# Capsule passes 2 and 3 of a graph network: half of the step sums added by VectorE from PSUM, and another layout of a chunk's edges

## What is computed

```python
xc = l2norm(x.reshape(num_node, 8, 16))
z = xc[src]
u = xc
for _ in range(3):
    p = einsum('ecd,ecd->ec', z, u[trg])
    p = softmax(p, axis=1)
    msg = z * p[:, :, None]
    u = segment_sum(msg, trg, num_segments=num_node)
    u = l2norm(u + xc)
```

## Time and profile before

| what | value |
|---|---|
| median of 3 runs | 6134.75 us (6134.14 to 6145.96) |
| span of the profiled execution | 6133.4 us |
| median less that span | 1.35 us |
| `CAPS2` and `CAPS3` in it | from 3089 to 4062 us of the span, 488 steps |
| POOL busy over the span | 4562.7 us (74%) |
| PE busy | 3912.3 us (64%) |
| DVE busy | 3726.0 us (61%) |
| ACT busy | 1638.9 us (27%) |

### The profile page before, as it was taken

One profiled execution on the slowest core, in us unless ns is written; L12 is line 12 of the kernel. 1 busy time (PEld: TensorE's weight loads), 2 busy tenths in 40 slices (PEclk: granted clock), 3 DMA queues, 4 the chain that ended last, 5 costly groups with the idle time before them and its releaser, 6 DMA issues. The chain is left out here.

```text
span 6133.4 us, 123500 instructions
## 1 busy us (share of the span) xinstructions
PE 3912.3 (64%) x27584; PEld 3400.1 (55%) x27585; DVE 3726.0 (61%) x9157; ACT 1638.9 (27%) x4058; POOL 4562.7 (74%) x5214
## 2 busy tenths in 40 slices
PE   1555555555555477777789989956566665666665
PEld 1544444455455366666578878845555553555553
DVE  6333333565666677777887787775555555555555
ACT  1000000112121333333455565531111113222222
POOL 6777777677777677777778888857777776777776
PEclk9666666666666688888899999977777776888887
DMA  4222222222222355555577777732222222222222
GB/s 124 68 70 68 70 69 68 62 69 68 70 68 70 103 175 171 172 170 171 169 231 248 249 226 248 249 109 69 69 69 69 70 68 54 71 71 71 69 71 95
DMA packets 447304, 697.73 MB, mean 114 GB/s; under 512 B 89485, under 2 KB 204570, under 8 KB 446282
## 3 DMA queue, kind: packets, MB, share of 16 engines
q0 software_dynamic: 127616, 263.32, 16.6%
q10 hardware_dynamic: 210816, 255.92, 12.8%
q1 hardware_dynamic: 108746, 177.24, 9.1%
HBM read 506.58 MB, written 189.53 MB: 113 GB/s over the span
## 5 line engine op out<-in xcount | busy, mean ns | idle before, releaser
L759 POOL DMA_INDIRECT u_parts<-table,src x3128 | 2951.6, 944 | 1063.2 <-issue 952.1
L835 PE MATMUL ps_sum<-u_parts,onehot 128*128 x2928 | 655.5, 395 | 691.6 <-SPq L588 552.2
L1374 DVE SCALAR_TENSOR_TENSOR onehot<-dst,minus_row,beside 128x512 f32<-128x512 f32 x1100 | 816.9, 744 | 365.7 <-issue 308.6
L835 PEld LDWEIGHTS ps_sum<-u_parts,onehot 128*128 128x128 f32 x2928 | 573.7, 291 | 776.2 <-issue 775.4
L759 POOL DMA_INDIRECT ring<-table,src x782 | 746.2, 954 | 264.9 <-issue 237.7
L835 PE MATMUL ps_u<-u_parts,onehot 128*128 x2928 | 535.9, 343 | 515.6 <-SPq L588 452.2
L835 PEld LDWEIGHTS ps_sum<-msg,onehot 128*128 128x128 f32 x4896 | 693.7, 213 | 306.8 <-issue 149.1
L835 PE MATMUL ps_sum<-msg,onehot 128*128 128x128 f32 x4896 | 753.9, 303 | 127.0 <-DVE msg L457 96.9
L835 PEld LDWEIGHTS ps_u<-u_parts,onehot 128*128 128x128 f32 x2928 | 473.0, 246 | 566.0 <-issue 565.0
L1669 DVE TENSOR_TENSOR zu<-ps_u,ring 128x512 f32<-128x512 f32 x732 | 502.7, 687 | 351.7 <-SPq L588 192.6
L885 PE MATMUL ps_u<-u_parts,hots 128*128 x5856 | 487.9, 235 | 56.2 <-ACT hots L1144 39.4
(11 more groups left out here) (205 smaller groups left out, 6477.8 us busy)
## 6 DMA issues: line engine op xcount, KB each, us to landing
ring<-z_rows SPq DMA_DIRECT2D x392, 256.0 KB, 3.5
hot_rows<-hots ACTq DMA_DIRECT2D x244, 256.0 KB
hots<-hot_rows ACTq DMA_DIRECT2D x244, 256.0 KB, 3.4
z_rows<-ring SPq DMA_DIRECT2D x196, 256.0 KB, 2.1
u_parts<-table,src POOLq DMA_INDIRECT x3128, 2.5
table<-hots ACTq DMA_DIRECT2D x122, 256.0 KB
wide<-hot_rows ACTq DMA_DIRECT2D x122, 256.0 KB, 3.4
wide_t<-hot_rows ACTq DMA_DIRECT2D x122, 256.0 KB, 3.5
```

The costliest lines, as they stand in the source:

```text
L759: nc.gpsimd.indirect_dma_start(out=slot(p, c % slots)[:, t * P:(t + 1) * P], out_offset=None, in_=tables[p], in_offset=bass.IndirectOffset ...
L835: last = nc.tensor.matmul(sums[k % len(sums)][:, 0:P], lhsT=(onehot[:, k % HOTS, :, :] if hots_of is None else hots_of)[:, t, :], rhs=rows ...
L1374: V.scalar_tensor_tensor(out=buffers[k % len(buffers)], in0=per_row(dst[:, ds(chunk * TILES, TILES)], [P, TILES, P]), scalar=minus_row0[:, ...
```

## The change

Of the step sums of `CAPS2` and `CAPS3`, POOL keeps the even steps (`pool_adds`). The odd ones are added by DVE straight from PSUM with `add_step`, in the even iterations, seven iterations behind (`lag` 3 becomes 7). ACT copies only the even sums and raises `sum_out` by 2; PE waits for `sum_out` before it refills an even bank, for `step_added` before an odd one. POOL's wait for the start of a piece of `x` now covers step s+1 too.

Apart from that, the host lays out a chunk's edges by tiles: edge number t·128 + p of a chunk goes to tile t, partition p, where before edge 4·p + t did. The last chunk holds 160 edges and gathers 2 tiles.

```diff
+        def pool_adds(k):
+            return k % 2 == 0
...
-                    if have(3):
+                    if have(3) and pool_adds(k - 3):
                         add(s.back(3), k - 3, chunk(3))
...
-                    if s.fixed and (s + 0) % PIECE == 0 and s + 0 < PIECES * PIECE:
-                        pool.wait_ge(acc_started, PIECES + thirds_before(m, (s + 0) // PIECE + 1))
+                    for first in (s + 0, s + 1) if s.fixed else ():
+                        if first % PIECE == 0 and first < PIECES * PIECE:
+                            pool.wait_ge(acc_started, PIECES + thirds_before(m, first // PIECE + 1))
...
-                                 step_added if p == CAPS1 else sum_out,
+                                 sum_out if p > CAPS1 and pool_adds(k - lag) else step_added,
...
-                    if have(4):
+                    if have(4) and pool_adds(k - 4):
                         act.wait_ge(step_summed, s + (G - 3))
                         act.wait_ge(step_added, s + (G - 7))
                         nc.scalar.activation(sums_out[k % len(sums_out)], four_sums[k % len(four_sums)][:, 0:P],
-                                             ACT.Copy).then_inc(sum_out, 1)
+                                             ACT.Copy).then_inc(sum_out, 2)
...
-                lag = SUM_LAG[p] + 2 if p == CAPS1 else 3
+                lag = SUM_LAG[p] + (2 if p == CAPS1 else 3)
...
+                    if p != CAPS1 and have(lag) and not pool_adds(k - lag):
+                        add_step(s.back(lag), k - lag, chunk(lag), p, caps_sums[p])
                     if s.fixed and s + 0 < STEPS:
                         piece_work(s, p)
...
-        return padded.reshape(CHUNKS, P, -1).transpose(1, 0, 2).reshape(P, -1)
+        return padded.reshape(CHUNKS, TILES, P).transpose(2, 0, 1).reshape(P, -1)
...
-        "attr": attr.reshape(CHUNKS // RING, RING, P, TILES * D_EDGE).transpose(0, 3, 1, 2)
+        "attr": attr.reshape(CHUNKS // RING, RING, TILES, P, D_EDGE).transpose(0, 2, 4, 1, 3)
```

## The result

The changed kernel takes **6150.7 us** (median of 10 runs, 6148.89 to 6151.71). The kernel before took 6135.52 beside it: ratio 1.0024, 95% interval 1.0016 to 1.0032, so slower by 15 us. The forecast was 6161, slower. The direction and the range held; the time was forecast 10 us too high.

A forecast was written before the change was run, and what follows sets the result against it. The loop was taken to be bound by a circle over prob_n, first message, PE, zu and reciprocal, without POOL's adds. Terms -7.0 + 5.6 + 9 + 7.0 + 7.5 + 4.7 = +26.8 us gave 6161; range 6110 to 6180, own case 6147 to 6178.

The forecast's parts named there:

- POOL's relief, loops: Loops of CAPS2 and CAPS3: fewer POOL adds help the slower circle 0.42 and 0.08 in 24 steps, -7.0 us.
- adds and table load at DVE's tops: At 28 tops of DVE's loop: adds 0.20 each, +5.6 us, and the longer table load 0.25 each, +7.0 us.
- adds, changes of passes: Where passes change DVE is 95% busy and has no gaps: 52 adds, 10.4 in full, taken as +9 us.
- loads, written-out rounds: Outside the loops 34 table loads grow from 8 to 12 values, and CAPS3 gets one more: +7.5 us.
- end of CAPS3: DVE must add step 243 before the next layernorm's statistics and 4.78 us of work: +4.7 us, bounds 3 and 5.
- slower circle: One of two interleaved circles of even and odd pairs, prob_n to reciprocal to prob_n: 6.90 us for four steps.
- On the slower circle this helps only where POOL was late: Loops: POOL's shorter pair gains only 0.42 at one pair and 0.08 at another in 24 steps, -7.0 us.
- the rival on POOL's pace: Loops: POOL sets the pace, 6 of 12 pairs gain 0.41 each, 35 us; total 6112 us, chance 0.21.
- Some lie behind a piece instruction: +7.5 of 9.4: Written-out rounds: some longer table loads hide behind a piece instruction on DVE, so +7.5 us of 9.4 counts.
- all exposed: Upper end of the forecast's own range, all adds and loads exposed and POOL's relief nothing: 6178 us.
- The adds hold each other: Rival: POOL's and DVE's alternating adds wait in order, 0.3 each on 244 adds, 73 us more: 6230 us, chance 0.05.
- The port: Rival: DVE's adds slow POOL's messages, 0.5 us each on 244, about 6250 us, chance 0.03.

The follow-up runs named there:

- e1: Changed kernel with the CAPS3 adds from step 236 on given back to POOL, run again on another chip: 7515.04 us against 7505.87 before, ratio 1.0013.
- a1: Kernel before with POOL's adds of the odd steps left out and none given to DVE: 6122.23 us, ratio 0.9979.
- c2: Kernel before with DVE's reciprocal of a pair put ahead of the logit of the same iteration: 7610.72 us against 7619.85, ratio 0.9987.
- e3: Kernel before with the pair's reciprocal moved ahead of logit in the loops alone: 7495.03 us against 7505.87, ratio 0.9985.
- a2: Kernel before with DVE's window of table values at 8 in place of 4 in CAPS2 and CAPS3: 6144.31 us, ratio 1.0015.
- a3: Kernel before with one more DVE add into unused space in every even iteration of CAPS2 and CAPS3 from the eighth on: 6145.51 us, ratio 1.0016.
- b2: Changed kernel with the sums of steps 236 to 243 of CAPS3 all added by POOL: 7626.5 us against 7619.85 before, ratio 1.0005.

## Why the prediction was right, point by point

| term | forecast | by itself | in the changed kernel |
|---|---|---|---|
| POOL's relief, loops | -7.0 | -15.1 | -11.5 |
| adds and table load at DVE's tops | +12.6 | +3.0 and +5.9 | +9.9 |
| loops together | +5.6 | -6.2 | -2.0 |
| adds, changes of passes | +9 | +6.3 | } |
| loads, written-out rounds | +7.5 | +2.5 | } +12.3 with the relief |
| relief there | 0 | +2.9 | } |
| end of CAPS3 | +4.7 | | +4.9 |
| sum | +26.8 | | +15.2 |

The -11.5 and +9.9 are those of the slower circle's intervals above, from step 42 to 210; the -2.0 is the lag from step 40 to 208.

**The direction** rested on three statements. The work was taken from an engine that the loop waits for little: that was half right, as the loop gains twice as much from the relief as forecast. It was given to one that has few gaps at the change of passes: that held, at six tenths of the full price. And the end, where DVE must now wait for PE's and POOL's last step, costs 4.9 us for 4.7 forecast, which e1 gave back in full. So the mechanism stood, and the sum was off by errors that mostly went the same way. The measured time lies only 4 us above 6147, the lower end of the forecast's own range.

**The tops of the loop** held too: an add that costs 0.20 and a load that grows by 0.25 were to lengthen 28 intervals by 0.45, and they grew by 0.31 to 0.52 in the patterns above, 0.38 on average. By themselves the two come to 8.9 us; why the adds alone are cheaper there, 3.0 for 5.6, no run shows.

**"On the slower circle this helps only where POOL was late"** is the first step that failed. The prediction counted the places where POOL's `prob_n` of that circle had no idle time before it, one in six and a little. But the pairs of the other circle, which it took to have room, pass their lateness on. At POOL's own table load (1.06 us from 3428.7) one of them begins 1.06 us behind the end of its reciprocal, 3429.04 to 3430.10, in place of 0.14, and in a1 the intervals of the slower circle beside it shrink by 0.31. What ties them is, I take it, PE, which does the sums of all steps in order with the `ps_u` of the next ones. Before, PE stood idle 0.52 us for that late pair's first message (until 3431.72), and at the same place of a1 (3426.24) it did not; but no run took that tie away by itself, so the link is argued, the 15.1 us are measured. The true price of POOL's adds lay between the forecast's 7 and the 35 of the rival on POOL's pace. The rival failed as well: c2 and e3 speed the loop up by as much with all of POOL's adds in place, by one reciprocal that comes earlier.

**"Some lie behind a piece instruction: +7.5 of 9.4"** is the second: the reason was right and the share was mis-sized, 2.5 us came out. The earlier trace rows gave the duration right, 0.60 to 0.85. But a longer load costs only where the engine runs out of work while it lasts: a2 has 4.2 us more of such idle time, not 8.5, and part of that is taken up by later waits. DVE's timeline of before would have told the rounds with a piece instruction, with no idle time beside the load at 3583.6, from those with 0.45 behind it, as at 3497.18. The same holds in part for the adds in the changes of passes: 6.3 of the 9.

**How the 11.6 us between 26.8 and 15.2 come about.** In the changed kernel the loops came out 7.6 us under the forecast (relief 4.5 more, tops 2.7 less), the changes of passes and the steps beside them 4.2 less, the end 0.2 more. The single runs explain the 4.2 only roughly: the adds 2.7 less, the loads 5.0 less, and against them 2.9 that no term had, since with POOL's adds left out a1 made the changes of passes longer. Why it did was not followed up. By place they fit worse than in sum. From step 218 of `CAPS2` to 32 of `CAPS3` the changed kernel lost 7.2 us, where a1, a2 and a3 have 4.1 together; in the last 24 steps of `CAPS3` it lost 2.4, where they have 4.3. There the terms don't simply add, and what they do to each other stays open.

Three sums of the prediction are off without touching the forecast. By its own terms, "all exposed" comes to 6172 us and not 6178, and the rival on POOL's pace, with half of all other costs, to 6119 and not 6112. The third stands below.

**The other rivals.** The adds hold each other: DVE's adds waited for POOL's three times in the two passes, 4.4 us, all at the end; POOL's waited for DVE's 35 times, 32.7 us. The rows of POOL's adds of both passes, what they waited for, and who waited for them:

```profile
  DVE x L1394: 32.7, 35
...
  DVE x L1394: 4.4, 3
```

In the loop this wait comes once at each top of DVE's, and there `prob_n` would have waited for DVE anyway (it starts 0.14 us behind the end of the reciprocal each time), so it costs nothing there. At the end it is part of the 4.9 us, which the prediction had as a term. The port: POOL's messages between 3400 and 3500, beside DVE's adds, are what they were the earlier trace rows:

```profile
L457 POOL TENSOR_TENSOR msg<-ring,prob_n x40: 1056/1057/1062, 3401.1 to 3499.4; 128x512 f32<-128x512 f32 x40
```

That is as the Trainium skill has it in SBUF — State Buffer, section Who interferes with whom, for a VectorE instruction with at most one input in SBUF; the trace agrees, at 1.057 us for the message. Of the 488 messages of the two passes 275 run beside an add; six take more than 1.1 us, all in the changes of passes, where before has eight. The other rule weighed was the overhead of an instruction on PSUM by the Trainium skill's Perfetto Trace Analysis, section Optimizing Scalar/DVE Operations, with the 0.26 us an add estimated from it. From the add's start to the next instruction's the trace has 0.20 (3587.75 to 3587.95, in the change of passes) and 0.26 (3406.77 to 3407.03, at a top). On the 80 adds that were priced, the 0.06 between the two would have made an estimated 4 to 5 us more, and not the 2 to 3 of the prediction: away from the 15.2 measured.

## What to carry to other kernels

Where two interleaved circles share an in-order engine, don't price a relief on the slower circle alone: find every place where the relieved engine is late, on either, and take a part of each. A longer table load is priced by the idle time beside it in the engine's timeline, not by its own duration. Here it cost nearly in full behind a loop's branch, 5.9 of 7.0 us, and 2.5 of 8.5 in straight code: mostly nothing beside a large instruction, all 0.25 where the shorter load had only just been covered. And before work is moved off an engine, ask which single small instruction on the circle stands behind one that it doesn't need: here moving one 0.2 us reciprocal ahead of a 0.69 us instruction gave 15.1 us over the two passes (e3), with every add left in place; leaving out half of POOL's adds gave 15.1 in the loops (a1).

## What the runs showed of the hardware

- A load of register values grows with their number: DVE 1.10 us for 16 values, 1.35 for 20; POOL 1.06 for 16, 1.79 for 28. Behind a loop's branch DVE's idle time grew by the whole difference, 1.44 to 1.69. In straight code a load of 0.85 us ran beside a large instruction with no idle time, and without one the idle time grew from 0.45 to 0.70 when the load went from 0.60 to 0.87.
- Halving the number of such loads with twice the loop length made the loop slower, 45.1 for 44.4 us in 24 steps, although the stalls at the loads themselves fell from 3.4 to 3.1 us.
- The kernel before took 6135, 7506 and 7620 us on three chips. The capsule passes kept their times: the changed kernel and its two copies with another end (b2, e1) take 970.3, 970.4 and 970.3 us from the first `prob_n` to the last.
